# Combining two experts per token: rows gathered from device memory in place of products with a turned combine matrix, under another instruction order

## The chip, the cores and the metric

The kernel is one launch on one core of a Trainium2 chip. The metric is the device time of that core in microseconds (us). TensorE is PE in the profile (its weight loads PEld), VectorE DVE, ScalarE ACT, GpSimd POOL and SyncE SP; SPq is SyncE's queue of DMA issues.

## The reference, cut to what matters

Four batches of 512 tokens of width 128 pass through two layers. Each layer is a cross attention (16 heads of width 8, at most 77 keys) with a residual, then a mixture of experts with a residual. The mixture of layer 0 is the one that changes:

```python
logits = jnp.einsum('gth,he->gte', xg, w_router)         # 8 groups of 256 tokens, 8 experts
probs = softmax(logits); _gate, idx = top_k(probs, 2)
# place in the expert's queue: all first choices of the group count before the second ones
priority = jnp.cumsum(expert_mask, axis=1) * expert_mask - 1
dispatch = one_hot(priority, 64)                         # 64 places for each expert and group
combine = probs[..., None] * dispatch
expert_in = einsum('gth,gtec->gech', xg, dispatch)
h = gelu(einsum('gech,ehf->gecf', expert_in, wi))        # 128 -> 512
expert_out = einsum('gecf,efh->gech', h, wo)             # 512 -> 128
out = einsum('gech,gtec->gth', expert_out, combine)
```

A token of group g thus receives the sum of at most two rows of `expert_out`, each times the router's probability of its expert, and nothing for a choice whose place is past 64. Layer 1's mixture has 8 dense experts without places (and two null experts); it is unchanged.

## The kernel before

The work is cut into 8 runs: run 0 to 3 are the batches in layer 0, run 4 to 7 the same batches in layer 1. A run has NT = 4 tiles of 128 tokens; tiles 0 and 1 are one group of the router, tiles 2 and 3 the other. All work is float32 but for the one-hot matrices and the three bf16 parts into which `split_x` cuts the tokens.

**The attention of a tile** is a chain over all engines: `attn_scores` (PE, L1008, and the mask's L1012), `softmax_max` (DVE: the bias added, L1640, and the maximum of each head, L1642), `shift` (POOL: the maximum subtracted, L408), `softmax_exp` (ACT, L624), `turn` (PE transposes, L1027), `copy_PT` (ACT, L632), `weigh_values` (PE, L1046), `invert` and `normalise` (DVE, L1647, L1652), `project` (PE, L1052), `add_residual` (DVE, L1659). Two buffers `SC` alternate, so two tiles are under way at once.

**The mixture of layer 0**, once for each batch: router logits (PE), some 16 small DVE steps (softmax, best and second best expert, each counted by the semaphore `m_route`), `positions` (PE), `own_position`, `slot` and `slots` (DVE: the 0/1 matrix `Dm`, L1776). `dispatch` (PE) collects the tokens of each expert's places into `ein`. `up` (PE, L1135, 8 experts) and `gelu` (ACT, L653) alternate on one PSUM bank; `down` (PE, L1150) gives the expert rows of two experts at a time, which `copy_eo` (ACT, L658) puts in `eo`: four blocks k of 128 rows (two experts by 64 places) by two groups by 128.

To combine, `combine_weights` (POOL, L454) multiplies `Dm` by the probabilities, once for each tile; `turn_C` (PE, L1125) turns the result in four 128 by 128 transposes; `copy_CT` (ACT, L646) brings it out of PSUM; `combine` (PE, L1158) is four products of 128 by 128 for each tile; and `add_mixture` (DVE, L1815) adds the PSUM bank to `X`. The next layer's `a_stats` and `residual_bias` of that batch wait for it.

**The mixture of layer 1** is `logits1`, 24 small DVE steps, `expert_bias` (PE) and `start_acc` (DVE, L1828), then for each tile `experts` (PE, L1210), `weigh_expert` (DVE, L1847, 4 experts), `scale_experts` (ACT, L670, the 4 others) and `sum_experts` (POOL, L440, L442, L445).

**The order** on each engine is written out by hand as a list of calls, one list for each engine, with the work of run r's attention between the mixture steps of earlier batches: while run 2 is in its attention, PE does `up(0, ...)`, while run 3, `up(1, ...)`, and so on to `up(3, ...)` in run 5. Engines run their lists in order; semaphores join them. SyncE's list is all loads, with those of masks and biases of later batches waiting until their buffers are free, and then the stores of the result. The last loads are:

```python
            for a in range(2, B):
                for g in range(2):
                    load_mask(a, g)
                    load_bias(a, g)      # waits: added >= (a - 1) * NT + 2 * (g + 1)
```

An ACT instruction that needs another table of functions (`Exp` in `softmax_exp` and `route_exp`, `Gelu_apprx_tanh` in `gelu`) than the one before it is preceded by an ACT_TABLE_LOAD.

Of the kernel before, what the change touches and what calls it, by code (L numbers as in the profile page):

```python
# [8 lines left out]
U8 = mybir.dt.uint8  # L9
ALU = mybir.AluOpType  # L10
# [3 lines left out]
P = 128  # L14


def bass_xattn_moe_twice(nc, x, ctx_in, bias, attn_mask, mask, pad_mask,
# [30 lines left out]
    ROUTE0, ROUTE1 = 18, 24  # L48

    ctx = ExitStack()  # L50
    with ctx:
# [6 lines left out]
        def sem(name):  # L58
# [9 lines left out]
        rank = sb("rank", [P, NG])  # L68
        half = sb("half", [P, NT])
# [70 lines left out]
        Cm = shared[:].rearrange("p (n e c) -> p n e c", n=2, e=NE)  # L140
        CT = sb("CT", [P, NT, NE // 2, P])
# [27 lines left out]
        m_logits m_route m_exp m_cum m_split m_D m_C m_disp m_eins m_CT m_CTs m_h m_hs m_eo m_eos m_comb m_out  # L169
# [36 lines left out]
        def _(sp):  # L206
# [69 lines left out]
            def store(f):  # L276
                b = f - B
# [15 lines left out]
        def _(pool):  # L293
# [50 lines left out]
            def numbers():  # L344
# [3 lines left out]
                       allow_small_or_imprecise_dtypes=True).then_inc(s["c_ok"], 1)  # L348

# [21 lines left out]
            def residual_bias(a, layer):  # L371
# [48 lines left out]
            def split_x(f):  # L420

                pool.wait_ge(s["f_xnok"], NT * (f + 1))
                if f > 0:
                    pool.wait_ge(s["m_disp"], 2 * f)
                base = 4 * f
# [8 lines left out]
            def sum_experts(f, i):  # L434

                n = NT * (f - B) + i
# [10 lines left out]
            def combine_weights(f, i):  # L447

                if f == 0 and i == 0:
                    pool.wait_ge(s["k_v"], B)  # L450
                pool.wait_ge(s["m_D"], 2 * f + i // 2 + 1)
# [1864 lines left out]
```

## Time and profile before

| | |
|---|---|
| median of 3 runs | 375.06 us (374.32 to 375.06) |
| profiled execution: first to last instruction | 371.0 us |
| around the span, by the median | 4.1 us |
| instructions | 8972 |
| TensorE busy | 318.2 us, 86% |
| VectorE busy | 261.1 us, 70% |
| GpSimd busy | 183.1 us, 49% |
| ScalarE busy | 173.2 us, 47% |

The profile is one execution. Its span runs from the first to the last instruction; launch and end lie outside it. A busy share is an average over stretches that have different limits, so the stretches have to be looked at one by one. "Idle before" in a row is the time that the engine sat idle ahead of those instructions, and the name behind the arrow is what ended it.

### The profile page before, as it was taken

The numbers are of one execution on the slowest core, as the hardware profiler recorded it, in microseconds if no ns is written. First come the engines' busy times: TensorE is split into PE (matmuls) and PEld (weight loads), VectorE is DVE, ScalarE is ACT, GpSimd is POOL, SyncE is SP. The second block draws the span as 40 slices with busy tenths as digits, with TensorE's granted clock in tenths as the row PEclk, the third lists the DMA queues.
The fourth block names the chain that finished last, engine by engine and source line by source line (L and its number), as shares of the span: only waits on it lengthen the run. The fifth ranks groups of instructions, "written<-read, shape, count | busy, mean of one in ns | idle before, by whom it ended". The sixth has DMA issues, their size and how long they took to land.

```text
span 371.0 us, 8972 instructions
## 1 busy us (share of the span) xinstructions
PE 318.2 (86%) x3628; PEld 237.4 (64%) x3633; DVE 261.1 (70%) x639; ACT 173.2 (47%) x321; POOL 183.1 (49%) x197
## 2 busy tenths in 40 slices
PE   3789767899999999999999999999787987798771
PEld 2468465577888778778788778885444653556420
DVE  4669665977596396852679566667779689986762
ACT  3144313375844827349285464735341363346331
POOL 7356283785708357163364714155362266624515
PEclk9999977999999999999999999999976699689995
DMA  7994970050504000000000000000000000000000
GB/s 191 256 374 107 333 213 2 2 145 3 138 10 113 27 2 2 3 2 2 2 3 2 2 2 2 3 0 2 3 0 31 0 3 0 30 2 3 0 28 28
DMA packets 26427, 19.15 MB, mean 52 GB/s; under 512 B 1973, under 2 KB 24339, under 8 KB 26387
## 3 DMA queue, kind: packets, MB, share of 16 engines
q1 hardware_dynamic: 26387, 18.59, 17.3%
q8 instruction: 29, 0.48, 0.5%
q14 instruction: 11, 0.09, 0.1%
HBM read 17.53 MB, written 1.05 MB: 50 GB/s over the span
## 4 chain that ended last, share of the span: by engine, by line
PE 50%; DVE 25%; issue 10%; ACT 7%; POOL 6%; DMA 1%; POOLq 0%; DVEq 0%; ACTq 0%
PE PB L1046 9%; DVE SC L1640 6%; PE HBK L1135 6%; PE SP L1027 5%; PE SP L1008 4%; PE EBK L1150 4%; POOL SC L408 4%; DVE mx L1642 3%; ACT PT L632 3%; DVE acc L1847 3%; DVE rc L1647 3%; PE HBK L1210 2%; PE SP L1012 2%; PE HBK L1158 2%; PE EBK L1210 2%
## 5 line engine op out<-in xcount | busy, mean ns | idle before, releaser
L408 POOL TENSOR_TENSOR SC<-SC,mx 128x1232 f32<-128x1232 f32 x32 | 74.0, 2313 | 98.9 <-DVE mx L1642 98.8
L632 ACT COPY PT<-SP 128x512 f32<-128x512 f32 (+1 forms) x96 | 44.5, 526 | 44.5 <-PE SP L1027 38.4
L624 ACT ACTIVATE SC<-SC 128x1232 f32<-128x1232 f32 x32 | 39.4, 1234 | 26.8 <-POOL SC L408 26.7
L1027 PE MATMUL SP<-ident,SC 128*128 128x128 f32 x320 | 47.2, 292 | 4.6 <-ACT SC L624 4.0
L1642 DVE TENSOR_REDUCE mx<-SC 128x16 f32<-128x1232 f32 x32 | 46.0, 1436 | 1.1
L1027 PEld LDWEIGHTS SP<-ident,SC 128*128 128x128 f32 x320 | 39.1, 151 | 10.8 <-ACT SC L624 6.2
L1647 DVE RECIPROCAL rc<-PB 128x128 f32<-128x128 f32 x32 | 30.5, 954 | 21.0 <-PE PB L1046 20.7
L1135 PE MATMUL HBK<-ein,wi_s 128*128 128x128 f32 x256 | 36.1, 284 | 2.1 <-ACT hT L653 2.1
L1135 PEld LDWEIGHTS HBK<-ein,wi_s 128*128 128x128 f32 x256 | 31.1, 191 | 7.5 <-ACT hT L653 4.9
L1008 PE MATMUL SP<-KB,qT 32*128 32x308 f32 x256 | 28.8, 512 | 8.1 <-DVE SC L1640 4.3
L1046 PE MATMUL PB<-PT,VB 128*32 128x128 f32 x768 | 30.1, 294 | 5.7 <-ACT PT L632 4.9
L653 ACT ACTIVATE hT<-HBK 128x512 f32<-128x512 f32 x32 | 19.1, 597 | 30.2 <-PE HBK L1135 30.1
L1150 PE MATMUL EBK<-wo_s,hT 128*64 128x128 f32 x512 | 31.5, 276 | 0.6 <-DVE r_c L1762 0.5
L1046 PEld LDWEIGHTS PB<-PT,VB 128*32 128x32 f32 x768 | 21.1, 116 | 14.6 <-issue 8.1
L454 POOL TENSOR_TENSOR shared<-Dm,r_p 128x512 f32<-128x512 bf16 x16 | 16.5, 1043 | 27.2 <-DVE Dm L1776 21.9
L1150 PEld LDWEIGHTS EBK<-wo_s,hT 128*64 128x64 f32 x512 | 27.7, 137 | 3.4 <-issue 1.7
L1640 DVE TENSOR_TENSOR SC<-SP,BI 128x1232 f32<-128x1232 f32 x16 | 23.0, 1436 | 8.8 <-PE SP L1012 8.6
L1046 PE MATMUL PB<-PT,rowmask 128*32 128x128 f32 x768 | 29.0, 286 | 0.0
L1640 DVE TENSOR_TENSOR SC<-SP,amp 128x1232 f32<-128x1232 f32 x16 | 22.9, 1433 | 5.9 <-PE SP L1008 5.9
L670 ACT ACTIVATE hT<-EBK,cw 128x128 f32<-128x128 f32 x52 | 14.9, 378 | 19.0 <-PE EBK L1210 15.6
L1046 PEld LDWEIGHTS PB<-PT,rowmask 128*32 128x32 f32 x768 | 23.6, 116 | 0.0
L1008 PEld LDWEIGHTS SP<-KB,qT 32*128 32x128 f32 x256 | 11.5, 202 | 18.7 <-issue 7.8
(188 smaller groups left out, 569.7 us busy)
## 6 DMA issues: line engine op xcount, KB each, us to landing
BI<-in_fside_Bx16xSxS SPq DMA_DIRECT2D x8, 1232.0 KB, 6.6
wi_s<-in_L_ffn_wi SPq DMA_DIRECT2D x1, 2048.0 KB, 8.9
X<-in_x SPq DMA_DIRECT2D x4, 256.0 KB, 4.3
out<-acc SPq DMA_DIRECT2D x3, 256.0 KB, 2.2
MI<-in_mask_BxSxS_ik SPq DMA_DIRECT2D x8, 77.0 KB, 5.0
ew_s<-in_L_ffn_expert_w SPq DMA_DIRECT2D x1, 512.0 KB, 4.1
out<-acc SPq DMA_DIRECT2D x2, 128.0 KB, 1.7
ctxn<-in_ctx SPq DMA_DIRECT2D x1, 154.0 KB
```

The lines of the kernel that those rows point to most:

```text
L408: g.tensor_tensor(S4, S4, m4, ALU.subtract).then_inc(s["shifted"], 1)
L624: sc.activation(S3, S3, ACT.Exp).then_inc(s["probs"], 1)
L632: sc.copy(PT[:, c0:c1, :].rearrange("p c t -> p (c t)"), SP[:, n, 0:(c1 - c0) * P]).then_inc(s["PTs"], 1)
L653: sc.activation(hT[e % 4][:].rearrange("p c g s -> p (c g s)"), HBK[:], ACT.Gelu_apprx_tanh)\
L1008: last = te.matmul(SP[:, r4, 0:HQ * J], qT[rows, i * P:(i + 1) * P], KB[rows, a].rearrange("p h j -> p (h j)"), start=True, stop=(layer == 1))
L1027: last = te.transpose(SP[:, n, (c - c0) * P:(c - c0 + 1) * P], SC[i % 2][:, c * P:(c + 1) * P], ident[:])
L1046: last = te.matmul(PB[32 * q:32 * (q + 1), m * P:(m + 1) * P], w, PT[:, c, :], start=(k == mine[0]), stop=(k == mine[-1]))
L1135: last = te.matmul(HBK[:, c * P:(c + 1) * P], wi_s[:, e, c * P:(c + 1) * P], ein[:, e].rearrange("p g c -> p (g c)"), start=True, stop=True)
L1150: last = te.matmul(EBK[q * CAP:(q + 1) * CAP, g * D:(g + 1) * D], hT[(2 * k + q) % 4][:, c, g, :], wo_s[:, 2 * k + q, c, :], start=(c == 0 ...
L1640: v.tensor_tensor(o, i0, i1, ALU.add).then_inc(s["added"], 1)
L1642: v.tensor_reduce(mx[i % 2][:].rearrange("p (u h) -> p u h", u=2), heads_of(S_), AX.X, ALU.max)\
L1647: v.reciprocal(rc[:], PB[:, P:2 * P]).then_inc(s["recips"], 1)
```

## The change

`combine_weights`, `turn_C`, `copy_CT` and `combine` are gone, and with them `Cm` and `CT`. The expert rows are stored to a device memory buffer `slab` of 1024 rows by 128 (row number 256 k + 2 p + g), four stores of 128 KB for each batch, issued by SyncE behind all of its loads. DVE works out for each token and choice the row number and the gate, in five small steps. POOL issues 32 indirect DMAs (4 batches, 4 tiles, 2 choices), each of which fetches one row of 512 bytes for each of 128 tokens into `G`, which takes the memory of `Cm`. ACT multiplies by the gates, POOL adds the two choices, and DVE adds the sum to `X`:

```diff
+            def keep(f, k):
+                b = batch_of(f)
+                sp.wait_ge(s["m_eos"], NE // 2 * b + k + 1)
+                if b > 0 and k == 0:
+                    for i in range(NT):
+                        sp.wait_ge(s[f"m_got{i}"], 32 * b)
+                sp.dma_start(slab.rearrange("(k p g) d -> k p g d", k=NE // 2, g=2)[k], eo[:, k]).then_inc(s["m_kept"], 16)
...
-            def combine_weights(f, i):
+            def gather(f, i):
+                b = batch_of(f)
+                if i == 0:
+                    pool.wait_ge(s["m_kept"], 16 * NE // 2 * (b + 1))
+                    pool.wait_ge(s["m_route"], ROUTE0 * b + 22)
+                if b > 0 and i == 0:
+                    pool.wait_ge(s["m_out"], b + 1)
+                for k in range(2):
+                    g.indirect_dma_start(out=G[:, i, k, :], out_offset=None, in_=slab,
+                                         in_offset=bass.IndirectOffsetOnAxis(ap=rows[:, i, k:k + 1], axis=0),
+                                         bounds_check=NE * CAP * 2 - 1, oob_is_err=False).then_inc(s[f"m_got{i}"], 16)
+
+            def add_choices(f):
+                pool.wait_ge(s["m_weighed"], NT * (batch_of(f) + 1))
+                g.tensor_tensor(G[:, :, 0, :], G[:, :, 0, :], G[:, :, 1, :], ALU.add).then_inc(s["m_sum"], 1)
...
             def copy_eo(f, k):
+                if batch_of(f) > 0 and k == 0:
+                    act.wait_ge(s["m_kept"], 16 * NE // 2 * batch_of(f))
+            def weigh_choices(f, i):
+                act.wait_ge(s[f"m_got{i}"], 32 * (batch_of(f) + 1))
+                act.wait_ge(s["m_route"], ROUTE0 * batch_of(f) + 23)
+                for k in range(2):
+                    ins = sc.activation(G[:, i, k, :], G[:, i, k, :], ACT.Identity, scale=gate[:, i, k:k + 1])
+                ins.then_inc(s["m_weighed"], 1)
...
             def up(f, e):
                 if e == 0:
-                    pe.wait_ge(s["m_CTs"], NT * f + NT)
+                    pe.wait_ge(s["m_eins"], 2 * batch_of(f) + 2)
...
+            def position(f):        # r_w: sum of r_c over the experts
+            def within(f):          # r_h = min(r_w, CAP) * 2
+            def of_expert(f):       # r_b = r_s2 * (-2 * CAP) + r_h
+            def row(f):             # rows = r_b + rowbase, as uint32
+            def gates(f):           # gate = (r_w <= CAP + 0.5) * r_m2
...
             def add_mixture(f):
-                dve.wait_ge(s["m_comb"], f + 1)
-                v.tensor_tensor(xo, xo, HBK[:], ALU.add).then_inc(s["m_out"], 1)
+                dve.wait_ge(s["m_sum"], batch_of(f) + 1)
+                v.tensor_tensor(xo, xo, G[:, :, 0, :], ALU.add).then_inc(s["m_out"], 1)
```

`dispatch` no longer waits for `m_out` of the batch before. `weighed`, `pairs` and `xres` get memory of their own in place of shared memory. The lists of all five engines are written anew; what runs is otherwise the same. The part of POOL's list around the gathers, and of ACT's and PE's lists, as they stand after:

```python
# POOL
shift(2, 3) mask_out(3, 0) mask_out(3, 1) gather(0, 0) gather(0, 1) shift(3, 0) gather(0, 2) gather(0, 3)
f_rstd(2) shift(3, 1) add_choices(0) a_rstd(4) residual_bias(3, 0) split_x(2) shift(3, 2) shift(3, 3)
gather(1, 0) gather(1, 1) gather(1, 2) gather(1, 3) shift(4, 0) add_choices(1) shift(4, 1)
...
shift(5, 1) f_rstd(4) gather(2, 0) gather(2, 1) gather(2, 2) gather(2, 3) shift(5, 2) ... add_choices(2)
... shift(5, 3) gather(3, 0) gather(3, 1) gather(3, 2) shift(6, 0) gather(3, 3) shift(6, 1) f_rstd(5) add_choices(3)
# PE, run 5 to the end of run 7's attention
weigh_values(5, 3) expert_bias(4) attn_scores(6, 1, 1) experts(4, 0) ...
weigh_values(6, 3) expert_bias(5) attn_scores(7, 1, 1) experts(5, 0) experts(5, 1) ...
weigh_values(7, 3) expert_bias(6) project(7, 3, 1) experts(6, 0) experts(6, 1) experts(6, 2) f_xTr(7) ...
```

Before, `expert_bias(4)` and `experts(4, 0)` and `(4, 1)` stood in run 5, and `expert_bias(6)` and `experts(6, 0)` and `(6, 1)` in run 7. ACT's list changes between `Exp` and `Gelu_apprx_tanh` 25 times after and 19 times before.

## Rows read from the trace of the kernel before

**Rows 1.** The page, part 1: busy us, share of the span, instructions.

```profile
PE 318.2 (86%) x3628; PEld 237.4 (64%) x3633; DVE 261.1 (70%) x639; ACT 173.2 (47%) x321; POOL 183.1 (49%) x197
```

**Rows 2.** Busy time of each engine by stretch, cut at the runs' last add_residual.

```profile
core 0: us, PE busy (x) PEld busy (x) DVE busy (x) ACT busy (x) POOL busy (x), PEclk, DMA share, GB/s
0.00:51.80 51.80, 36.82 (x407) 26.49 (x408) 35.35 (x85) 16.92 (x30) 27.97 (x43) 0.99 0.85 249
51.80:89.50 37.70, 33.58 (x382) 26.24 (x383) 28.21 (x67) 16.30 (x28) 22.84 (x22) 0.88 0.21 57
89.50:132.50 43.00, 42.49 (x565) 35.25 (x566) 26.85 (x67) 27.17 (x42) 21.65 (x20) 1.00 0.23 63
132.50:181.60 49.10, 46.67 (x598) 38.66 (x602) 33.09 (x61) 27.02 (x44) 22.68 (x19) 1.00 0.01 2
181.60:224.30 42.70, 41.38 (x551) 34.13 (x549) 29.36 (x68) 24.87 (x40) 23.76 (x19) 1.00 0.01 2
224.30:264.40 40.10, 37.43 (x486) 30.27 (x485) 26.77 (x76) 21.62 (x40) 13.55 (x13) 1.00 0.01 2
264.40:306.70 42.30, 35.28 (x310) 21.50 (x310) 34.71 (x88) 15.89 (x36) 20.03 (x22) 0.80 0.02 8
306.70:344.40 37.70, 29.93 (x304) 19.23 (x303) 31.46 (x74) 15.94 (x35) 19.59 (x22) 0.86 0.03 8
344.40:371.00 26.60, 14.59 (x39) 5.66 (x38) 15.30 (x59) 7.46 (x27) 11.07 (x20) 0.82 0.06 20
```

**Rows 3.** Groups by line and shape: busy us, mean ns | idle before.

```profile
L653 ACT ACT_TABLE_LOAD x9 | 11.5, 1283 | 0.2
L1158 PE MATMUL HBK<-W,CT 128*128 128x128 f32 x128 | 15.2, 276 | 0.0
L1125 PE MATMUL HBK<-ident,shared 128*128 128x128 f32 x32 | 4.9, 277 | 0.1
L454 POOL TENSOR_TENSOR shared<-Dm,r_p 128x512 f32<-128x512 bf16 x16 | 16.5, 1043 | 27.2 <-DVE Dm L1776 21.9 <-PE HBK L1125 4.8 <-PE EBK L1125 0.5
L646 ACT COPY CT<-EBK 128x512 f32<-128x512 f32 x8 | 4.8, 602 | 2.1 <-PE EBK L1125 2.1
L670 ACT ACTIVATE hT<-EBK,cw 128x128 f32<-128x128 f32 x52 | 14.9, 378 | 19.0 <-PE EBK L1210 15.6 <-POOL hT L440 3.4
L428 POOL TENSOR_TENSOR acc<-f_xn,xh 128x512 f32<-128x512 f32 x4 | 4.6, 1161 | 0.3
```

**Rows 4.** Waits, longest total first: us in total, times, longest.

```profile
POOL SC L408 <- DVE mx L1642: 98.8, 22, 11.2
```

**Rows 5.** Single lines' instructions: ns min/median/max, first and last start.

```profile
L408 POOL TENSOR_TENSOR SC<-SC,mx x32: 2242/2249/3232, 15.9 to 333.5; 128x1232 f32<-128x1232 f32 x32
L363 POOL TENSOR_TENSOR a_rs<-a_ve,half x8: 1037/1042/1865, 5.2 to 299.2; 128x4 f32<-128x4 f32 x8
L1708 DVE TENSOR_TENSOR r_l<-MB,r_m x4: 191/192/193, 59.4 to 190.4; 128x32 f32<-128x32 f32 x4
```

**Rows 6.** POOL in order of time: start, us, instruction, idle before.

```profile
181.14 2.25 POOL L408 TENSOR_TENSOR SC<-SC,mx 128x1232 f32<-128x1232 f32 x1 [11.23 <-DVE mx L1642]
...
243.23 2.25 POOL L408 TENSOR_TENSOR SC<-SC,mx 128x1232 f32<-128x1232 f32 x1 [10.21 <-DVE mx L1642]
```

**Rows 7.** DMA issues: KB each, median us to landing; the last load in SyncE's queue.

```profile
BI<-in_fside_Bx16xSxS SPq DMA_DIRECT2D x8, 1232.0 KB, 6.6
out<-acc SPq DMA_DIRECT2D x2, 128.0 KB, 1.7
115.72 0.38 SPq L230 DMA_DIRECT2D BI<-in_fside_Bx16xSxS  x1
```

**Rows 8.** PE in order of time, layer 1's experts near the end.

```profile
344.23 1.02 PE L1210 MATMUL HBK<-ew_s,f_xT 128*128 128x512 f32 x2
346.86 1.12 PE L1210 MATMUL HBK<-ew_s,f_xT 128*128 128x512 f32 x2 [0.74 <-DVE acc L1847]
```

**Rows 9.** DVE in order of time: the last add_mixture.

```profile
247.10 0.69 DVE L1815 TENSOR_TENSOR X<-X,HBK 128x512 f32<-128x512 f32 x1
```

More of the change, by code:

```diff
@@ L47, in bass_xattn_moe_twice, with layer_of, batch_of, run_of @@
     LAYERS = 2
-    ROUTE0, ROUTE1 = 18, 24
+    ROUTE0, ROUTE1 = 23, 24
+    RUNS = ((0, 0), (0, 1), (0, 2), (0, 3), (1, 0), (1, 1), (1, 2), (1, 3))
+    def layer_of(run):
+        return RUNS[run][0]
+    def batch_of(run):
+        return RUNS[run][1]
+    def run_of(layer, b):
+        return RUNS.index((layer, b))
+    def mixtures_before(f):
+        return sum(layer == 0 for layer, b in RUNS[:f])
     ctx = ExitStack()
@@ new lines, in _ @@
+            gather(1, 0)
+            gather(1, 1)
+            gather(1, 2)
+            gather(1, 3)
+            shift(4, 0)
+            add_choices(1)
+            shift(4, 1)
+            f_rstd(3)
+            a_rstd(5)
+            residual_bias(4, 1)
+            shift(4, 2)
+            shift(4, 3)
+            split_x(3)
+            mask_attn(5)
+            shift(5, 0)
+            shift(5, 1)
+            f_rstd(4)
+            gather(2, 0)
+            gather(2, 1)
+            gather(2, 2)
@@ L541, in _ @@
+            gather(2, 3)
+            shift(5, 2)
+            block_keys(2, 1, "k_kb1")
+            add_choices(2)
             residual_bias(5, 1)
@@ L780, in _ @@
             softmax_exp(3, 3)
[L781 to L783 removed]
+            gelu(2, 0)
             copy_PT(3, 3, 0)
             copy_PT(3, 3, 1)
[L786 removed]
             gelu(2, 1)
+            weigh_choices(1, 0)
             gelu(2, 2)
+            weigh_choices(1, 1)
+            weigh_choices(1, 2)
             gelu(2, 3)
+            softmax_exp(4, 0)
+            weigh_choices(1, 3)
+            copy_eo(2, 0)
+            copy_PT(4, 0, 0)
@@ L1927, in _ @@
             f_norm(1, 0)
-            softmax_max(2, 1, 0)
+            position(0)
+            invert(2, 0)
+            softmax_max(2, 2, 0)
+            within(0)
+            of_expert(0)
+            row(0)
+            gates(0)
             logit_max(1)
@@ L2055, in _ @@
             f_norm(4, 1)
-            softmax_max(5, 1, 1)
+            invert(5, 0)
+            normalise(5, 0)
+            softmax_max(5, 2, 1)
+            softmax_max(5, 3, 1)
+            add_mixture(2)
+            a_stats(6, 1)
             gate_logits(4)
+            add_residual(5, 0, 1)
+            of_expert(3)
+            row(3)
+            gates(3)
             logit_max(4)
```

1186 lines of the change are left out of this document (575 added, 611 removed).

## The prediction

> **What bounds the kernel now.** I read the page first: TensorE is busy 86% of the span, the fullest of the engines [rows 1]. An average hides stretches with different limits, so next I cut the span at the end of each run's attention and asked for the busy time of every engine in each stretch [rows 2]. The reader is to see three regimes. Runs 1 to 5 (51.8 to 264.4 us, 212.6 us together) are TensorE's: it is busy 33.58 + 42.49 + 46.67 + 41.38 + 37.43 = 201.6 us of them, 94.8%, and 96% in runs 2 to 5, while DVE has 144.3 us (68%). Runs 6 and 7 are nobody's alone: TensorE 83% and 79%, DVE 82% and 83%, and one run takes 42.3 and 37.7 us. Here the softmax chain passes from engine to engine. The last 26.6 us are the tail of layer 1's mixture, with TensorE and DVE both a little over half busy.
>
> A busy matmul row can be a pipelined one that hides room, so I read the removed work in wall time: the 128 products of `combine` occupy 15.2 us with no idle time before them, about 3.8 us for each batch, in TensorE's fixed order [rows 3]. Whatever stands behind them waits for that.
>
> The Trainium skill (Perfetto Trace Analysis, "Identifying the Most-Contended Engine") says that matmul busy share is no good measure of nearness to the peak, and that the share of weight loads should be read. By that share, some 79% in runs 2 to 5, a fifth of TensorE's time would be free and the removal worth a fifth less, some 5 us; the sum below does not use it.
>
> **Removed from TensorE.** The 128 products, 15.2 us. The 64 transposes of `turn_C`: the row shown has 32 of them at 4.9 us, its twin on the other bank as many, 9.8 us [rows 3]. Together 25.0 us, all in runs 1 to 5. That leaves 176.6 us of TensorE work there. Two tiles of `experts` also leave run 5 for later, four pairs of products at 1.02 us [rows 8], and `expert_bias(4)`, which I count as one and a half such pairs: 171 us left.
>
> How densely can that be packed? With 94.8% as before the five runs take 180.5 us. But DVE keeps its 144.3 us and gets five small steps for each batch, 20 x 0.19 = 3.8 us [rows 5]: 148 us. At 180 us that is 82% for DVE, as much as it reaches in runs 6 and 7, where TensorE falls to 83%. With both engines loaded, the density comes out between the two regimes. I take 92%, since TensorE is still the fuller one: 171 / 0.92 = 186 us, a gain of 26.6 us over these runs. At 83%, as in run 6, it would be 206 us, a gain of 6.6 us. These are the two bounds, 32 and 6.6 us.
>
> **Given back in the tail.** In runs 6 and 7 as many layer 1 tiles are worked on as before (eight, batches 4 and 5 in place of half of 4, all of 5, half of 6). The tail gets two more tiles and `expert_bias(6)` with `start_acc(6)`. One tile costs 2.6 us there (346.86 - 344.23 us [rows 8]), so 5.3 us, and the bias with `start_acc`, which I count at most of another, 2 us; a little of it hides under `f_norm(7)` and routing's chain of small DVE steps. I charge 6 us (bounds 3 and 9).
>
> **ACT.** Sixteen `copy_CT` of 0.60 us go (the row shown has 8 of them at 4.8 us): -9.6 us. Thirty-two gate multiplications of 128x128 come, at the 0.378 us of `scale_experts` [rows 3]: +12.1 us. Six more table loads of 1.283 us: +7.7 us. Net +10 us. ACT is busy 54% in runs 1 to 5 (117.0 of 212.6 us [rows 2]), 68% afterwards, so the cover is ACT's idle time; a table load in front of `softmax_exp` or a `gelu` delays TensorE's next `turn` or `up` though, and I charge 2 us of the 7.7. Without cover it would be the whole 10.
>
> **POOL.** Sixteen `combine_weights` go, 16.5 us. Four `add_choices` of 128x512 come at 1.16 us (the nearest row is L428), 4.6 us [rows 3]. The 32 gathers are the unknown: no POOL queue DMA is in this trace. Below, an issue of a DMA by SyncE takes 0.38 us [rows 7]; above, POOL's heaviest instruction takes 2.25 us [rows 5]. A gather works through 128 numbers, one for each partition, most like the 128x4 power of L363 at 1.04 us [rows 5]. I take 1.05 us, 34 us in all; POOL then has 183 - 16.5 + 4.6 + 34 = 205 us, 58% of the new span. Its share is no problem; its place is. POOL is in the softmax chain, and eight gathers in a row (8.4 us) stand ahead of `shift(4, 0)` and of `shift(5, 2)`, six ahead of `shift(6, 0)`, four on each side of `shift(3, 0)`. Queued behind them is the shift, and for it wait `softmax_exp`, `turn` and `weigh_values`. What hides them is that POOL already sits waiting for DVE before its shifts: 98.8 us over 22 waits, the longest 11.2 [rows 4], among them 11.23 and 10.21 us just where TensorE does `up` and `down` [rows 6]. So 8.4 us fit, with under 2 us to spare. I charge 1 us for stretching: DVE and POOL can hold each other up, as the longest shift at 3.23 against 2.25 us and a power at 1.87 against 1.04 us show [rows 5].
>
> The Trainium skill (SBUF, "Who interferes with whom") says that a GpSimd DMA's descriptors are written by GpSimd through ports that DVE's two-port modes lock. By it, gathers beside `a_norm` or `f_norm` would stretch; it is the mechanism of the slower case below, and no row here shows a gather. The same skill (DMA: Bandwidth & Descriptors, "Latency and other measured facts") gives about 1 us to the first byte of such a DMA; 32 of them would be 32 us, which is an estimate from the page.
>
> **Stores, landing, DVE.** `keep` stands in SyncE's queue behind the last `load_bias`, which goes out at 115.72 us, when tile 3 of run 2 is added [rows 7]. Nothing but the later stores is behind `keep`. Its four 128 KB stores land in 1.7 us each when alone, and in up to 6.6 us behind the bias load. A gather lands between the same bounds. `gather(0, 0)` stands behind `shift(2, 3)`, 4 us after that load went out, so it waits perhaps 3 us more, ahead of a `shift(3, 0)` whose scores aren't ready. The path from the last `copy_eo` to `add_mixture` becomes store 2, eight gathers 8, landing 2, gates 3 and sum 1.2 us, some 16 us in place of `combine`'s 4. Nothing of the layer 1 run of that batch is due for most of a run: mixture 3 is added at 247.1 us before [rows 9], and the attention that needs it begins when run 6's ends, at 306.7 us [rows 2]. So I cost it at nothing; if the cover were gone it would be 12 us, once. `add_mixture` itself is as before. The beginning is reordered too: 51.8 us with DMA 85% busy and TensorE at 71% [rows 2]. I take no change, within 3 us.
>
> **The sum.** 371.0 - 26.6 + 6 + 2 + 1 = 353.4 us of span. Around the profiled span lie 375.06 - 371.0 = 4.1 us to the median of the runs, so about 357.5 us. I say 358.
>
> **Rivals.**
>
> The whole gain is kept: the packing stays at 94.8% and the tail takes 3 us more. 371 - 32 + 3 + 1 + 4.1, some 348 us. For it, runs 2 to 5 reach 96% although they are interleaved in the same manner; against it, DVE at 82%.
>
> TensorE's freed time turns into waits, and its clock falls with them. The granted clock is 1.00 in runs 2 to 5, where TensorE is 93 to 99% busy, but 0.88 in run 1 at 89% and 0.80 in run 6 at 83% [rows 2]; those are shares of time at 1.2 in place of 2.4 GHz. Packing at 83 to 88% leaves 6.6 to 18 us, less 9 us for the rest: 366 to 377, likeliest 369.
>
> No change that can be measured (within 0.2%, 0.75 us, which is what this kernel's measurement can tell): the same mechanism at its lower end.
>
> The other side: the gathers delay the shifts. Each block of eight takes 8g against a wait of 10.2 us. Over four blocks the loss is 4 x (8g - 10.2), which reaches the forecast gain of 17.5 us at g = 1.8 us, and decides from there. At the upper bound of 2.25 us it is 31 us: 389 us. For it: in-order POOL, tight margins, stretched neighbours. Against it: the nearest row at 1.04 us, and blocks for batches 0 and 3 that are split by a shift.
>
> **How the numbers follow.** Forecast, 352 to 365 us: 0.52. Whole gain: 0.10. Waits and clock, still faster: 0.18. Same: 0.05. Slower 0.15: the gathers above 1.8 us 0.12, the waits' upper end 0.03. So faster 0.80, same 0.05, slower 0.15. Range 347 to 377 us: it leaves out the far part of the slower case (about 0.1) and little below. The likeliest case alone has 352 to 365.
>
> **What would show it.** Runs 2 to 5 of 37 to 39 us each, TensorE at 90% or more in them; gathers near 1 us on POOL and waits before the shifts of runs 4 and 5 cut from 10 to about 2 us; a tail of some 32 us; granted clock at 1.00 until run 5 ends. A tail over 36 us, a clock under 0.95 in the middle, or gathers of 1.8 us and more would make the forecast wrong.

## The result and the profile after

The changed kernel takes **370.0 us** (median of 4 runs, 368.65 to 371.52) beside 374.7 for the kernel before on the same chip: ratio **0.9884** (95% interval 0.9847 to 0.9921). On another chip, in 6 runs, it came to 369.7 us and 0.9889 (0.9845 to 0.9933). It is faster, as predicted, and inside the range, but by 1.2% where I forecast 4.5%.

The profiled execution spans 369.8 us; it is the slowest of the four (371.5 us), so the two profiles lie only 1.2 us apart where the medians lie 4.7. First the page's part 1 of it, to be read beside [rows 1], then the busy times by stretch, cut as in [rows 2] at the runs' last `add_residual`:

```profile
PE 304.4 (82%) x3441; PEld 224.1 (61%) x3441; DVE 286.0 (77%) x659; ACT 182.3 (49%) x343; POOL 200.8 (54%) x218
```

```profile
core 0: us, PE busy (x) PEld busy (x) DVE busy (x) ACT busy (x) POOL busy (x), PEclk, DMA share, GB/s
0.00:59.60 59.60, 44.03 (x395) 31.56 (x395) 40.32 (x93) 18.60 (x34) 30.10 (x46) 0.95 0.78 220
59.60:95.30 35.70, 32.10 (x428) 25.63 (x429) 31.66 (x66) 17.36 (x25) 18.92 (x19) 0.99 0.30 81
95.30:139.00 43.70, 40.04 (x532) 32.60 (x530) 32.58 (x65) 28.94 (x43) 22.14 (x20) 0.96 0.21 61
139.00:186.60 47.60, 40.91 (x517) 33.01 (x515) 37.63 (x73) 27.92 (x53) 26.79 (x24) 0.93 0.09 27
186.60:231.00 44.40, 37.54 (x469) 30.79 (x470) 35.86 (x71) 25.99 (x41) 20.75 (x16) 0.88 0.04 13
231.00:274.00 43.00, 36.80 (x479) 29.06 (x477) 32.26 (x78) 25.00 (x51) 30.73 (x29) 0.96 0.14 39
274.00:311.90 37.90, 31.48 (x313) 19.19 (x313) 36.58 (x91) 17.13 (x41) 23.86 (x28) 0.95 0.03 8
311.90:336.20 24.30, 20.71 (x270) 14.48 (x270) 21.91 (x63) 11.58 (x27) 13.17 (x15) 0.93 0.04 12
336.20:369.80 33.60, 20.82 (x47) 7.74 (x47) 17.19 (x67) 9.74 (x35) 14.32 (x26) 0.76 0.05 16
```

Set the lengths against [rows 2], stretch by stretch. The start takes 7.8 us more. Runs 1 to 5, where all the products stood, take 214.4 us against 212.6: **by these borders they gained nothing**. Runs 6 and 7, which the products never touched, take 62.2 us against 80.0. The tail takes 7.0 us more. 7.8 + 1.8 - 17.8 + 7.0 = -1.2 us, which is 371.0 - 369.8. In runs 2 to 5 TensorE is busy 155.3 of 178.7 us, 87% where it was 96%, and its granted clock is 0.88 to 0.96 where it was 1.00. DVE has 25 us more in all.

These borders hide a part of it, because the new order moved work across them. When run 5 ends, 24 row maxima have been taken before, those of runs 0 to 5 and no more, but 26 after: the scores and maxima of run 6's first two tiles now stand inside run 5, and run 7's stretch holds only two of its four. Here are the 6th and the 26th row maximum on VectorE, first before, then after:

```profile
48.26 1.44 DVE L1642 TENSOR_REDUCE mx<-SC 128x16 f32<-128x1232 f32 x1
275.16 1.44 DVE L1642 TENSOR_REDUCE mx<-SC 128x16 f32<-128x1232 f32 x1
```

```profile
55.08 1.44 DVE L1659 TENSOR_REDUCE mx<-SC 128x16 f32<-128x1232 f32 x1
271.00 1.44 DVE L1659 TENSOR_REDUCE mx<-SC 128x16 f32<-128x1232 f32 x1
```

Counted this way, with equal numbers of tiles, the start is 6.8 us later, the 20 tiles in the middle take 215.9 us (216.7 in e16) against 226.9, **11.0 us less**, the last six take 6.3 us less (the 32nd starts at 332.02 and 321.60 us), and what is behind them 9.2 us more; the sum is again -1.2. So the middle gained between nothing and 11 us, by what is counted, and a good part of the 17.8 us of runs 6 and 7 is work that now stands in front of them or in the tail.

The chain of work that ended last (part 4 of the page) says which engines the time went through. TensorE had 50% of it before, VectorE 25% and GpSimd 6%. After:

```profile
DVE 35%; PE 24%; issue 18%; POOL 15%; ACT 3%; SPq 2%; DMA 1%; POOLq 0%; DVEq 0%; ACTq 0%
```

The gathers alone are 6% of it, some 22 us.

Where DVE's 25 us come from, by groups (line, engine, tiles, count, busy us, mean ns, idle before):

```profile
L496 POOL DMA_INDIRECT shared<-slab,rows x32 | 32.8, 1025 | 14.6 <-issue 8.6 <-DMA slab<-W 5.9
L1605 DVE TENSOR_SCALAR a_xn<-X,a_mv,a_rs 128x128 f32<-128x128 f32 x32 | 18.3, 638 | 0.4 <-POOL a_rs L399 0.4
L1605 DVE TENSOR_SCALAR f_xn<-X,f_mv,f_rs 128x128 f32<-128x128 f32 x32 | 18.0, 623 | 5.5 <-POOL f_rs L399 5.4
L1855 DVE TENSOR_TENSOR X<-X,shared 128x512 f32<-128x512 f32 x4 | 5.9, 1483 | 3.0 <-POOL shared L503 3.0
L1792 DVE TENSOR_SCALAR r_h<-r_w 128x8 f32<-128x8 f32 x4 | 4.6, 1148 | 0.0
L714 ACT ACTIVATE shared<-shared,gate 128x128 f32<-128x128 f32 x32 | 10.2, 396 | 1.8 <-DMA shared<-slab,rows 1.8
```

The two norms took 25.0 us before and take 36.3; the mixture's addition took 2.7 and takes 5.9 (its second input was in PSUM and is now in SBUF); `within` (L1792), a step on 8 numbers for each partition, takes 1.15 us in the mean. These aren't longer instructions but instructions that were held. One of them, in DVE's order of time, and the shift beside it in GpSimd's:

```profile
171.19 0.28 DVE L1676 TENSOR_TENSOR X<-PB,xr 128x128 f32<-128x128 f32 x1
171.39 2.24 DVE L1792 TENSOR_SCALAR r_h<-r_w 128x8 f32<-128x8 f32 x1
173.66 0.17 DVE L1796 SCALAR_TENSOR_TENSOR r_b<-r_s,r_h 128x8 f32<-128x8 f32 x1
```

```profile
171.35 2.25 POOL L445 TENSOR_TENSOR SC<-SC,mx 128x1232 f32<-128x1232 f32 x1 [12.13 <-DVE mx L1659]
173.77 1.16 POOL L496 DMA_INDIRECT shared<-slab,rows  x1 [0.17 <-issue]
175.23 1.01 POOL L496 DMA_INDIRECT shared<-slab,rows  x1 [0.30 <-issue]
...
183.05 1.00 POOL L496 DMA_INDIRECT shared<-slab,rows  x1 [0.31 <-issue]
184.08 2.26 POOL L445 TENSOR_TENSOR SC<-SC,mx 128x1232 f32<-128x1232 f32 x1
```

`within` begins 0.04 us after the shift and ends 0.03 us after it. Take all DVE instructions that lasted over 0.5 us more than the shortest of their line and shape, and sum what they lasted more: 7.9 us before and 35.4 after, 28.6 of them beside a shift. (The expectation of e3 has 11.6, 41.0 and 30.7, which this rule doesn't give.) The new order puts norms and routing steps right behind `softmax_max`, whose end is what starts the shift. The Trainium skill (SBUF, "Who interferes with whom") says that a DVE instruction with two SBUF inputs, or one in a two-port mode, and a GpSimd instruction that reads SBUF exclude each other entirely; by that rule, the trace agrees (2.24 us for 8 elements).

The same rows show the gathers: 1.00 us each and 0.30 between two, so eight take 10.3 us and not the 8.4 of the prediction. The first shift of run 4 stands behind them and starts at 184.08 us. Its row maximum was there at 182.07.

### The profile page after: what moved, and what is told of

Same layout as the page of the kernel before. It is cut to its first block, busy times and chain, and to the rows that moved or that the text cites. A ratio compares the mean times of both kernels' runs of the same rounds, so it can differ in the third digit from the quotient of the medians.

```text
span 369.8 us, 8712 instructions
## 1 busy us (share of the span) xinstructions
PE 304.4 (82%) x3441; PEld 224.1 (61%) x3441; DVE 286.0 (77%) x659; ACT 182.3 (49%) x343; POOL 200.8 (54%) x218
## 3 DMA queue, kind: packets, MB, share of 16 engines
q0 software_dynamic: 1024, 2.10, 2.2%
## 4 chain that ended last, share of the span: by engine, by line
DVE 35%; PE 24%; issue 18%; POOL 15%; ACT 3%; SPq 2%; DMA 1%; POOLq 0%; DVEq 0%; ACTq 0%
DVE SC L1657 7%; POOL shared L496 6%; PE PB L1099 5%; POOL SC L445 5%; DVE mx L1659 4%; DVE a_xn L1605 3%; DVE acc L1887 3%; DVE f_xn L1605 3%; PE SP L1080 3%; DVE rc L1664 3%; PE SP L1061 2%; PE HBK L1251 2%; PE EBK L1200 2%; DVE X L1855 1%; PE SP L1065 1%
## 5 line engine op out<-in xcount | busy, mean ns | idle before, releaser
L445 POOL TENSOR_TENSOR SC<-SC,mx 128x1232 f32<-128x1232 f32 x32 | 72.0, 2250 | 93.6 <-DVE mx L1659 93.5
L1080 PE MATMUL SP<-ident,SC 128*128 128x128 f32 x320 | 44.5, 287 | 9.4 <-DVE SC L1657 4.8
L1080 PEld LDWEIGHTS SP<-ident,SC 128*128 128x128 f32 x320 | 38.1, 148 | 17.3 <-ACT SC L675 9.0
L496 POOL DMA_INDIRECT shared<-slab,rows x32 | 32.8, 1025 | 14.6 <-issue 8.6
L1200 PE MATMUL EBK<-wo_s,hT 128*64 128x128 f32 x512 | 33.9, 289 | 0.0
L1200 PEld LDWEIGHTS EBK<-wo_s,hT 128*64 128x64 f32 x512 | 30.0, 145 | 3.0 <-issue 1.6
L1657 DVE TENSOR_TENSOR SC<-SP,BI 128x1232 f32<-128x1232 f32 x16 | 22.8, 1427 | 10.9 <-PE SP L1065 10.9
L1099 PE MATMUL PB<-PT,rowmask 128*32 128x128 f32 x768 | 30.9, 298 | 0.1
L1657 DVE TENSOR_TENSOR SC<-SP,amp 128x1232 f32<-128x1232 f32 x16 | 22.9, 1430 | 7.2 <-PE SP L1061 7.2
L1099 PEld LDWEIGHTS PB<-PT,rowmask 128*32 128x32 f32 x768 | 24.7, 121 | 0.6 <-issue 0.4
L725 ACT ACTIVATE weighed<-EBK,cw 128x128 f32<-128x128 f32 x52 | 14.8, 368 | 18.7 <-PE EBK L1251 15.2
L1605 DVE TENSOR_SCALAR f_xn<-X,f_mv,f_rs 128x128 f32<-128x128 f32 x32 | 18.0, 623 | 5.5 <-POOL f_rs L399 5.4
## 6 DMA issues: line engine op xcount, KB each, us to landing
wi_s<-in_L_ffn_wi SPq DMA_DIRECT2D x1, 2048.0 KB, 10.3
```

What stands on the lines that cost most here:

```text
L445: g.tensor_tensor(S4, S4, m4, ALU.subtract).then_inc(s["shifted"], 1)
L496: g.indirect_dma_start(out=G[:, i, k, :], out_offset=None, in_=slab, in_offset=bass.IndirectOffsetOnAxis(ap=rows[:, i, k:k + 1], axis=0), ...
L1080: last = te.transpose(SP[:, n, (c - c0) * P:(c - c0 + 1) * P], SC[i % 2][:, c * P:(c + 1) * P], ident[:])
L1099: last = te.matmul(PB[32 * q:32 * (q + 1), m * P:(m + 1) * P], w, PT[:, c, :], start=(k == mine[0]), stop=(k == mine[-1]))
L1200: last = te.matmul(EBK[q * CAP:(q + 1) * CAP, g * D:(g + 1) * D], hT[(2 * k + q) % 4][:, c, g, :], wo_s[:, 2 * k + q, c, :], start=(c == 0 ...
L1605: v.tensor_scalar(xn[:, i, :], x_of(run, layer)[:, i, :], mv[:, i, 0:1], rs[:, i:i + 1], ALU.subtract, ALU.mult).then_inc(s[pre + "_xnok"], 1)
```

## The experiments

All are timed in 5 rounds beside the kernel before; the ratios are what to compare.

**The start.** e1 puts the start of all four lists back in the order of before. e7 is e1 with `a_rstd(2)` and `a_rstd(3)` behind run 1's first two shifts, and VectorE's statistics and norm of runs 2 and 3 moved to suit. e9 is e8 (below) with two calls put back, of which this one, on VectorE, is in all three:

```diff
-spread_bv()
 scale_q(0, 0)
 softmax_max(0, 0, 0)
+spread_bv()
```

> The start of all four lists (to the end of run 0's attention) in the order of the kernel before, everything behind it as in the changed kernel. In the changed kernel run 0 ended at 59.6 us against 51.8, because VectorE waits 4.8 us for the last value-bias column before it scales the first queries. Theory 'the start was lost': the 5 to 8 us come back whole, 370 falls to 363 to 365. Rival 'a later stage takes it back' (the runs behind are bound by loads, by held VectorE instructions or by the gathers, and not by when they begin): under 2 us, 368 to 370.

> The order of the start again (run 0 as in the kernel before), now with the third and fourth run's inverse deviations on GpSimd behind the second run's shifts, where they don't block them: in the first trial of this order that block alone made an 8.7 us wait at 52 us, run 0 ended at 63.8 and the time rose by 3 us. Theory 'what the start loses stays lost': run 0 ends at 53 to 56 against 59.9, and the time falls by 4 to 6 us to 364 to 366. Rival 'taken back later': 368 to 370.

> e8_gathers_spread (364.7) with only two calls of the start put back: the spreading of the value bias behind the first softmax_max, so that VectorE no longer waits 4.8 us for its column before it scales the first queries, and the turning of the second weights behind the first scores. Theory 'the start's loss is this wait': run 0 ends 3 to 5 us earlier (53 to 55 against 58.5) and the time falls by 3 to 5 us to 360 to 362. Rival 'loads and the work of two runs packed beside them set the end of run 1': run 0 ends earlier, run 1 takes as much longer, 364 to 366, as in e7_start_again (run 0 ended at 55.3, run 1 took 42.6 us against 35.6).

e1: 373.4 us, 0.9967 (0.9930 to 1.0003), outside both forecasts, run 0 to 63.8. GpSimd, in its order of time, says why:

```profile
54.49 0.23 POOL L395 TENSOR_SCALAR a_ve<-a_mv 128x4 f32<-128x4 f32 x1 [14.06 <-DVE a_mv L1593]
...
57.12 4.45 POOL L445 TENSOR_TENSOR SC<-SC,mx 128x1232 f32<-128x1232 f32 x2
```

`a_rstd(2)` waited 14 us for statistics that my list had put behind `softmax_max(1, 1)`, and run 1's first two shifts stood behind it. That tells nothing of the start, only what one misplaced call costs. e7: 371.6 us, 0.9896 (0.9852 to 0.9939). Run 0 ends at 55.3, and run 1 takes 42.6 (the rows are cut 0.3 us early):

```profile
0.00:55.00 55.00, 40.90 (x415) 29.02 (x415) 35.24 (x84) 18.37 (x34) 27.60 (x43) 0.98 0.85 238
55.00:97.60 42.60, 35.86 (x407) 26.57 (x408) 33.79 (x73) 17.04 (x26) 21.63 (x22) 0.82 0.25 67
```

In part this is work that has gone to run 1: of the nine VectorE instructions that run 0 has fewer, run 1 has seven (2.1 of the 5.1 us). Its 6th row maximum is 4.4 us earlier than the changed kernel's, and its 26th, at 271.01 us, isn't earlier at all. e9: 367.0 us, 0.9773 (0.9728 to 0.9817), run 0 to 57.9 against 58.5: the wait for the bias column cost nothing. The rivals hold: what an earlier start gains is taken back later. The 7.8 us at the end of run 0 are 95.3 - 89.5 = 5.8 us at the end of run 1 by these two profiles; other kernels with the changed opening have 92.4 to 94.6 us there, and those with the old one 90.0 to 91.5 (e12, e13, e5): 1 to 6 us.

**The gathers.** e2 takes them off GpSimd; e8 keeps them and spreads them (with e3's VectorE list below, and `pick(1, 1)` moved too); e18 is e8's GpSimd list alone; e10 drops the weighing.

```diff
-gather(f, 0..3)                                   # GpSimd, 8 indirect
+sp.dma_start(G[:, i, k, :], slab[(2 * i + k) * P:(2 * i + k + 1) * P, :])   # e2, SyncE
```

```diff
 shift(5, 0)
+gather(2, 0)
 shift(5, 1)
 f_rstd(4)
-gather(2, 0)
 gather(2, 1)
-gather(2, 2)
-gather(2, 3)
 shift(5, 2)
+gather(2, 2)
+gather(2, 3)
...
+shift(5, 3)
 a_rstd(6)
```

> The indirect gathers are taken off GpSimd: in their place SyncE's queue fetches fixed rows of the slab into the same tiles with plain transfers, behind the same waits (the rows that the routing chose are left out, so the mixture is made of other rows). Theory 'the gathers on GpSimd cost the time': they occupy it for 1.30 us each, 10.3 us for a batch, with shifts of batches 4 and 5 2.0 and 5.2 us late: 7 to 12 us come back, 358 to 363. Rival 'GpSimd has that time to spare, the loss is on VectorE and at the start': at most 3 us, 367 to 370.

> The reordered VectorE list (e3_dve_unheld, 366) and beside it GpSimd's list: the eight gathers of batch 2 no longer in one row before shift(5,2) but one pair ahead of shift(5,1), one before shift(5,2) and two behind it, the last pair of batch 3 into the 6.6 us wait before shift(6,0), and shift(5,3) ahead of the next run's inverse deviations. Theory 'a row of gathers delays the shift behind it': 2 to 4 us come off, 362 to 364. Rival 'the shift is not what ends last there': 365 to 367.

> e8_gathers_spread once more (0.9717 before). e15_repairs, three moves away from it, came to 0.9833, which no theory of mine gives. If both are right, this comes to 363 to 366; if single executions at the start make the difference, 365 to 368.

> The changed kernel with GpSimd's list of e8_gathers_spread alone; VectorE's list is untouched. Theory 'a row of gathers delays the shift behind it by 5 us and this is paid': 2 to 3 us less than e16, 366 to 368. Rival 'only the VectorE order counts': within 1 us of e16.

> The changed kernel, in its own order, with the gathers, but without ScalarE's 32 weighings (12.1 us of it; the gate weights are left out of the result), the sum waiting for the gathers themselves. It divides the 12.7 us that lie between the changed kernel and the one without any mixture; the gathers' place on GpSimd is 5.3 of them. Theory 'the rest is ScalarE': 7 us come off, 362 to 364. Rival 'the rest is the transfers' landing and GpSimd's sum, ScalarE has room': at most 2 us, 368 to 370.

e2: 364.9 us, 0.9743 (0.9710 to 0.9776), 1.4 points below the changed kernel, some 5 us: between the rival's 3 at most and the theory's 7 to 12. GpSimd's share is real but small: its waits before the shifts grew from 93.5 to 126.0 us in e2, so nearly all of the gathers' 32.8 us turned into waiting, and only 5 us into time saved. Not all of the 5 need be GpSimd's time: these fetches also land in 1.9 us where the gathers take 2.6, and GpSimd's list no longer holds them back. e18: 367.8 us, 0.9830 (0.9792 to 0.9868), beside e16's 0.9889 on the same chip: 2 us, at the edge of what the intervals tell apart. e8: 364.7 us, 0.9717 (0.9684 to 0.9751), and again as e17: 364.9 us, 0.9770 (0.9732 to 0.9807). In GpSimd's order of time, first the changed kernel, then e8:

```profile
233.18 1.16 POOL L496 DMA_INDIRECT shared<-slab,rows  x1 [0.18 <-issue]
...
242.45 0.99 POOL L496 DMA_INDIRECT shared<-slab,rows  x1 [0.30 <-issue]
243.46 2.27 POOL L445 TENSOR_TENSOR SC<-SC,mx 128x1232 f32<-128x1232 f32 x1
```

```profile
227.95 1.16 POOL L496 DMA_INDIRECT shared<-slab,rows  x1 [0.19 <-issue]
229.42 1.01 POOL L496 DMA_INDIRECT shared<-slab,rows  x1 [0.30 <-issue]
233.11 2.25 POOL L445 TENSOR_TENSOR SC<-SC,mx 128x1232 f32<-128x1232 f32 x1 [2.68 <-DVE mx L1659]
235.51 1.02 POOL L496 DMA_INDIRECT shared<-slab,rows  x1 [0.15 <-issue]
```

The changed kernel's shift(5, 2) comes 5.2 us after its row maximum (238.27 us), e8's as soon as its own is there.

e10: 367.3 us, 0.9827 (0.9775 to 0.9879): 2 us less, but the intervals overlap. ScalarE had room for most of its 10.2 us.

**The held DVE steps.** e3 moves them away from the shifts (eight moves; two shown):

```diff
 invert(2, 0)
+within(0)
+of_expert(0)
+row(0)
+gates(0)
 softmax_max(2, 2, 0)
-within(0)
...
-add_mixture(1)
-a_stats(5, 1)
 softmax_max(4, 2, 1)
 f_norm(3, 0)
+add_mixture(1)
+a_stats(5, 1)
```

> Only VectorE's list: the routing steps of batches 0, 1, 2 and 3, three norms and the mixture's addition of batch 1 that stood right behind a softmax_max, and so beside GpSimd's 2.25 us shift, are moved a few places to stand before it or behind steps that read PSUM. In the changed kernel VectorE's instructions took 41.0 us more than their shortest, against 11.6 us in the kernel before, 30.7 of it beside a shift. Theory 'held VectorE steps are the loss': held time falls by 12 us or more and the time by 4 to 8 us, 362 to 366. Rival 'that time was slack on VectorE': held time falls, the time stays within 1 us of 370.

e3: 367.5 us, 0.9775 (0.9723 to 0.9827), 1.1 points, some 4 us below the changed kernel, where 4 to 8 were expected. Held time, counted as above, fell from 35.4 to 24.2 us, DVE's busy time from 286.0 to 276.3, and `within` of batch 2 is short again:

```profile
173.76 0.29 DVE L1676 TENSOR_TENSOR X<-PB,xr 128x128 f32<-128x128 f32 x1 [2.12 <-PE PB L1105]
173.97 0.36 DVE L1792 TENSOR_SCALAR r_h<-r_w 128x8 f32<-128x8 f32 x1
```

**The mechanism in the old order.**

```diff
-turn_C(f, i) / copy_CT(f, i) / combine_weights(f, i) / combine(f, n)
+gather(f, i) / weigh_choices(f, i) / add_choices(f) / position .. gates(f)
```

> The changed mechanism in the order of the kernel before: its four lists without the turned matrix and the products, with the gathers, the weighing, the sum and the row numbers put in beside where the products stood, and the mixture's addition moved behind them. It tells the mechanism from the searched order. Theory 'the mechanism is worth the forecast 4 per cent and the new order loses it': 355 to 362. Rival 'the mechanism itself is worth no more than 1 per cent, because its landing waits and GpSimd's time eat the products': 368 to 378, and the new order is worth something over this one.

e4: 406.9 us, 1.0861 (1.0823 to 1.0899): neither theory's. Runs 3 to 5 take 52.9, 50.5 and 59.8 us. Part of it is my places for the new calls. One run of waits, on ScalarE:

```profile
279.50 0.69 ACT L714 ACTIVATE shared<-shared,gate 128x128 f32<-128x128 f32 x2 [4.10 <-DMA shared<-slab,rows]
282.07 0.69 ACT L714 ACTIVATE shared<-shared,gate 128x128 f32<-128x128 f32 x2 [1.88 <-DMA shared<-slab,rows]
...
287.27 0.69 ACT L714 ACTIVATE shared<-shared,gate 128x128 f32<-128x128 f32 x2 [1.97 <-DMA shared<-slab,rows]
287.87 1.21 ACT L675 ACTIVATE SC<-SC 128x1232 f32<-128x1232 f32 x1
```

Four weighings wait for one landing after the other, at the pace at which GpSimd issues a tile's two gathers (2.6 us), with a `softmax_exp` behind them. TensorE waits 11.20 us for that `softmax_exp`, and DVE 12.66 us for TensorE. So e4 doesn't price the mechanism; it shows what it costs when an in-order engine asks for a fetch before it has landed.

**What the relief of TensorE is worth.** e5 is the kernel before with the combining left out, e6 the changed kernel with the storing, fetching, weighing and summing left out, and the waits for them. e12 and e13 cut the shift in the kernel before and in e5; e14 puts e3's order into e6.

```diff
-combine(f, n), turn_C(f, i), copy_CT(f, i), combine_weights(f, i)        # e5
-gather(f, i), weigh_choices(f, i), add_choices(f), keep(f, k)            # e6
+v.tensor_tensor(xo, xo, xo, ALU.max).then_inc(s["m_out"], 1)             # e5, e6: add_mixture
-g.tensor_tensor(S4, S4, m4, ALU.subtract)                                # e12, e13
+g.tensor_tensor(S4[:, 0:1, 0:1, :], S4[:, 0:1, 0:1, :], m4[:, 0:1, 0:1, :], ALU.subtract)
```

> The kernel before, in its own order, with the whole making of the mixture taken out and nothing put in its place (the products, the turned matrix, its copies and the gate weights on GpSimd; the addition stays with its place and about its price, so that the routed experts are left out of the result). It tests the term 'the 25.0 us that TensorE is relieved of come off the time'. My packing argument gives 375 less 25 to 27 = 348 to 350, with 16.5 us of GpSimd's time off as well. Rival 'runs 1 to 5 are a chain through VectorE, ScalarE and GpSimd, and TensorE's products filled its waits': 8 to 16 us come off, 359 to 367.

> The kernel before with GpSimd's shift cut to 77 of its 1,232 columns (the row maximum is left out of the other scores; waits and order stay), which takes about 2.1 us out of every row tile's chain and frees VectorE beside it. Theory 'TensorE's work packed tight bounds runs 2 to 5 here': at most 4 us come off, 371 to 375. Rival 'the chain through the shift bounds it even with the products': 10 us or more, 360 to 365.

> The same cut of the shift in the kernel before without any mixture (e5_before_no_mixture, 374.1), so that it tells whether what held that kernel at 374 with 25 us less on TensorE was the chain of a row tile. Theory 'chain': now the two gains come together, 15 us or more below e5, 350 to 359. Rival 'the fixed order of TensorE's list and its clock, not the shift': under 6 us, 368 to 374.

> The changed kernel, in its own order, without the stores to the slab, the gathers, the weighing and the sum (the addition keeps its place and price, the row numbers are still computed; the routed experts are left out of the result). It is what the changed kernel would take if the fetching cost nothing at all. Plain fetches in place of the gathers were already worth 5 us. Theory 'transfers, waits for their landing and the weighing on ScalarE cost little more': 362 to 365. Rival 'landing and ScalarE's 12.1 us of weighing stand in the way': 354 to 361.

> The changed kernel without the mixture (e6_after_no_mixture, 358.6) with VectorE's list of the unheld order. Theory 'held VectorE steps cost 4 us whatever the gathers do': 353 to 356. Rival 'they cost only where the gathers already press': 357 to 360.

e5: 374.1 us, **0.9972** (0.9935 to 1.0009). The whole combining is gone (the routing, `up`, `gelu` and `down` remain), and nothing gained, against a forecast of 25 us and a rival of 8 at least. Runs 2 to 5 of it:

```profile
91.20:132.60 41.40, 37.70 (x518) 29.78 (x517) 27.52 (x68) 25.17 (x38) 17.02 (x16) 1.00 0.24 65
132.60:178.60 46.00, 41.86 (x550) 33.28 (x552) 34.55 (x61) 25.02 (x40) 17.70 (x15) 1.00 0.01 2
178.60:224.30 45.70, 39.25 (x504) 30.95 (x501) 32.02 (x67) 22.93 (x37) 20.26 (x15) 0.89 0.01 1
224.30:268.70 44.40, 38.47 (x454) 28.91 (x454) 26.85 (x76) 21.56 (x40) 13.56 (x13) 0.88 0.01 2
```

They take 177.5 us against 174.9 [rows 2]. TensorE is busy 89% in place of 96%, and in runs 4 and 5 its granted clock is 0.89 and 0.88 in place of 1.00. Over the whole span 25.0 us of instructions left it, but it is only 11.2 us less busy (318.2 to 307.0), since the others take longer. GpSimd's wait before the shifts rose to 136.7 us from 98.8 [rows 4]. The profiled execution (375.9 us) is 1.9 us above the median, but the clock is low in all: 0.904 to 0.926 over the span in its 12 runs, 0.922 to 0.945 in 67 of the kernel before. Runs 2 and 3, at 1.00 in both, did gain, 87.4 us against 92.1; runs 4 and 5 lost more, 90.1 against 82.8. Where the clock falls, TensorE stands idle first, here until VectorE's `normalise` is there (PE in order of time, then 5 us from 200):

```profile
202.93 0.80 PE L1020 MATMUL PB<-WT,oT 128*128 128x128 f32 x2 [4.52 <-DVE oT L1596]
```

```profile
200.00:205.00 5.00, 2.07 (x9) 2.07 (x10) 4.96 (x4) 0.00 (x0) 2.24 (x2) 0.53 0.00 0
```

In run 5 the same follows a wait of 3.66 us that ends at 247.18.

e12: 369.1 us, 0.9791 (0.9742 to 0.9839), between its two forecasts. e13: 360.2 us, 0.9597 (0.9563 to 0.9632), some 14 us below e5 and just outside the theory's 350 to 359. Here runs 2 to 5 say more than the totals; first e12, then e13:

```profile
90.00:264.20 174.20, 167.57 (x2192) 138.07 (x2195) 113.00 (x269) 100.46 (x165) 52.21 (x69) 1.00 0.06 17
```

```profile
91.00:256.90 165.90, 150.27 (x2015) 119.60 (x2018) 111.05 (x270) 94.43 (x153) 38.96 (x57) 0.99 0.07 17
```

With the products, taking 2 us out of every row tile's chain leaves runs 2 to 5 where they were (174.2 against 174.9 us; e12's gain lies behind them). Without the products the same cut takes 177.5 to 165.9 us, and the clock is back at 0.99. So the kernel before stood at **two limits at once** in those runs: TensorE's work, and something that a shorter shift relieves. Relieved alone, neither gave anything.

What the second limit is, is shown less sharply. The row tile's chain through VectorE, GpSimd and ScalarE is the likely one, but the cut shift also frees VectorE (held time 11.0 us in e5, 1.6 in e13) and keeps the clock up, and these weren't taken apart. At a clock of 1.00 in both, runs 2 and 3 take 87.4 us in e5 and 85.9 in e13; nearly all of the gain lies in runs 4 and 5, 90.1 against 80.0, where the clock is 0.89 and 0.88 against 0.96 and 1.00. How much of the gain is the chain's and how much the clock's stays open.

e6: 358.6 us, **0.9544** (0.9501 to 0.9587), as the rival had it (354 to 361). Without the combining the new order is 4.3 points below the old one, and from the 6th to the 26th row maximum it takes 208.0 us where the old one takes 227.2. The new order with the products in it was never run, so what it is worth by itself isn't known. e14: 357.6 us, 0.9512 (0.9474 to 0.9550), not told apart from e6; what held steps cost where the combining is free stays open.

**Repairs together.** e11 adds to e9, and e15 to e8, `shift(3, 1)` ahead of `f_rstd(2)` on GpSimd, and `f_norm(2)` ahead of `softmax_max(3, 2)`; e15 also `shift(4, 0)` ahead of `gather(1, 3)`.

```diff
+shift(3, 1)
 f_rstd(2)
-shift(3, 1)
```

> e9_start_small with GpSimd's shift(3,1) ahead of the inverse deviations of batch 2, which waited for VectorE's statistics and held it back, and VectorE's norm of batch 2 again ahead of softmax_max(3,2), since it is no longer beside a shift there: TensorE waited 3.3 us for that norm. Theory: 2 to 3 us less than e9_start_small. Rival 'the wait moves to the softmax_max behind it': within 1 us of it.

> A version meant to beat both kernels: e8_gathers_spread (364.7) with shift(3,1) ahead of the inverse deviations of batch 2 on GpSimd, VectorE's norm of batch 2 ahead of softmax_max(3,2), and shift(4,0) ahead of the last pair of gathers of batch 1 (it was 2 us late behind them). If the shifts' lateness still counts, 361 to 364; if something else ends last there now, 364 to 366.

> The changed kernel once more, on the chip of the two runs beside it, so that the repairs are measured against it and not only against the kernel before. If its 0.9884 stands: 369 to 371. If it was measured too well or too badly there: outside of 367 to 373.

e11: 365.9 us, 0.9753 (0.9713 to 0.9792); e15: 368.6 us, 0.9833 (0.9782 to 0.9883). Neither beats e8: e11 is within 1 us of e9, as its rival said, and e15 is outside both of its forecasts. Why e15 is slower than e8 wasn't found; in its profile run 3 takes 49.3 us against 46.5. The best version is e8, the changed kernel with both repairs: beside e16 on the same chip 364.9 against 369.7 us, and 2.3 to 2.8% faster than the kernel before.

## Why the prediction was right and wrong

**The packing was the step that failed.** "171 / 0.92 = 186 us, a gain of 26.6 us over these runs": they took 214.4 us, 1.8 more than before, and counted by row maxima they gained 11.0. Both numbers of the quotient were off: TensorE is busy 187.4 us in place of 171, and 87% in place of 92%. The work shrank by 14 us and not by 30.6, since the clock fell (0.88 to 0.96 in runs 2 to 5, where it had been 1.00) and the fronts of two more tiles stand in these runs. I took the density of 96% as something that TensorE brings with it, and bounded it by a density seen elsewhere, 83%. But a density follows from the slower of two limits. The products filled waits; with them out, TensorE works less and waits more, and its clock falls with that. e5 shows it without any gather, and e13 shows that there is another limit, though not whether it is the chain itself or the clock that falls with its waits. My second rival had the mechanism ("TensorE's freed time turns into waits, and its clock falls with them", likeliest 369) and should have been the forecast. Of the signs named beforehand, runs 2 to 5 of 37 to 39 us (43.0 to 47.6) and a clock of 1.00 (0.88 in run 4) failed, while the gathers and the tail came as said. What would have told is that a run has another limit, and that nothing in the busy shares says how near it is: 98.8 us of GpSimd's waits before the shifts [rows 4] I read as cover for the gathers only, and not as a chain that comes round no sooner.

**The order was worth more than I gave it.** I held runs 6 and 7 equal, because the same number of expert tiles is worked on. They gave 17.8 us by their borders, but the fronts of two tiles and some of layer 1's experts have left them; from the 26th to the 32nd row maximum it is 6.3 us less. Their granted clock is 0.95 and 0.93 in place of 0.80 and 0.86 [rows 2]. e6 prices order and freed engines together at 4.6%, 17 us, though e5 gives freed engines alone nothing. That this is near my forecast (357.4 by its ratio, against 358) is chance: e5 takes the same work out of the old order and gains nothing.

**The fetch costs 12.7 us, not 3.** That is 0.9884 - 0.9544 = 3.4 points of 374 us; the forecast charged 1 us for GpSimd, 2 for ScalarE's table loads (which e6 has too), and nothing for landing, stores and weighing. Some 5 are the gathers' place on GpSimd (e2), 2 perhaps the weighing (e10, not certain), and the rest is not divided: landing, sum, stores and the waits for the slab. A gather at 1.03 us was forecast right (1.05); the 0.30 us between two was not, so that "under 2 us to spare" became 2.0 us late in run 4 and 5.2 us in run 5. That lateness didn't decide the time: e18's repair gives back 2 us.

**The "3.8 us" for DVE** was mis-sized: DVE rose by 24.9 us, and the time that its steps were held beside GpSimd by 27.5 us. The five new steps took 10.8 us with what they were held. I had seen such holding in GpSimd's longest instructions [rows 5] and charged 1 us. e3 shows that it is worth some 4 us.

**ACT** was sized right (10.2 us of weighing against 12.1, six table loads more), and its cover held but for some 2 us (e10). The table loads belong to the new order: e6, with no weighing, has 25 too. **The tail** was forecast at 6 us more and took 7.0. **The start**, taken as unchanged within 3 us, lost 1 to 6 by the end of run 1. The stores and the landing lay beside other work as said, except for one wait of 5.9 us of `gather(0, 0)` for the slab, since the last `copy_eo` of batch 0 came late, not because of the bias load in SyncE's queue.

Two slips in the prediction's arithmetic change nothing: the first rival's sum gives 347 us, not 348, and ACT's share in runs 1 to 5 is 55%.

## What to carry to other kernels

Before you price work taken off the busiest engine, take it out and put nothing in its place: if the time stays, a second limit stands beside the first, and a replacement must shorten that too. Look at the granted clock of both stretches before you call waits free. And before you compare stretches of two orders, count what stands in each: a border at the same call can have two more tiles' work in front of it. On an in-order engine a call's neighbours are part of its price: a step that GpSimd's instructions hold belongs behind steps that read PSUM, not right behind the step that starts GpSimd's long one. A new mechanism wants its own order; put into the old one, at the places that I chose, it lost 8.6%.

## What the runs showed of the hardware

An indirect gather of 128 rows of 512 bytes takes GpSimd 1.00 us (0.99 to 1.29 over all 32) and 0.30 us more before the next, and lands in 2.6 us. A GpSimd `tensor_tensor` on 128x1232 holds a DVE `tensor_scalar` from SBUF to SBUF, or a step with two SBUF inputs, to its own end, however small it is (0.16 us at the shortest, 2.24 held, for 128x8): of 16 that began beside a shift, 15 ended 0.02 to 0.09 us behind it and the longest 0.55. DVE steps with one input in PSUM aren't held: beside a shift, the 8 score additions of L1657 last 1.44 us at most and the 10 residual additions of L1676 0.29, as elsewhere. Nor are statistics and reductions from SBUF: `f_stats` lasts 0.30 us at most beside a shift. And TensorE's granted clock was 1.00, that is 2.4 GHz throughout, in runs 4 and 5 with the products, and 0.89 and 0.88 without them (e5), a mean over stretches at 2.4 and at 1.2 GHz: with the products it was busy 78.8 us there, without them 77.7.
